# A conditioning layer on one core: other orders on VectorE and ScalarE, a weight block summed by TensorE, a last row scale without GpSimd

## The reference

```python
h = _ln(x, pw_g[pathway_ids], pw_b[pathway_ids])      # a row of 500 for each token
h = _ln(h, cp_g[compartment_ids], cp_b[compartment_ids])   # a row of 5
t = _ln(x, tm_g[time_steps], tm_b[time_steps])        # a row of 5
m = x + _mlp_ln(memory_state, ...)[:, None, :]        # n, r alike, one row a batch
s = _ln(x, ms_g[scale_type], ms_b[scale_type])        # a row of 3
w = softmax(aw)
cat = concatenate([w[0]*h, w[1]*t, w[2]*m, w[3]*n, w[4]*r, w[5]*s])   # 3072 features
out = x + _mlp_ln(cat, int_W1, int_b1, int_W2, int_b2, int_g, int_be)
```

## Time and profile before

| | |
|---|---|
| median of 3 runs | 950.84 us (950.79 to 952.48) |
| the profiled execution | 952.21 us, span of its instructions 950.5 us |
| mean granted clock of TensorE | 0.997 of full |
| PE, PEld busy | 923.2 us (97%), 745.4 us (78%) |
| DVE busy | 825.8 us (87%) |
| ACT, POOL busy | 326.0 us (34%), 449.8 us (47%) |
| L1567, L1568, L1569 (PE) | 397.1, 393.1, 392.9 us, 1008 matmuls each |
| L842 h_write | 60 DMAs of 256 KB from ACT's queue |

### The profile page before, as it was taken

The page is one execution under the profiler, slowest core; times in us unless marked ns, Lnnn a source line. Parts: engine busy times, 40 slices in busy tenths (PEclk is TensorE's granted clock), DMA queues, the critical chain, the costliest instruction groups (busy, mean ns, idle before and its releaser), DMA issues.

```text
span 950.5 us, 13455 instructions
## 1 busy us (share of the span) xinstructions
PE 923.2 (97%) x4166; PEld 745.4 (78%) x4166; DVE 825.8 (87%) x1199; ACT 326.0 (34%) x415; POOL 449.8 (47%) x576
## 2 busy tenths in 40 slices
...
GB/s 327 353 296 142 207 170 254 168 127 247 125 235 162 192 217 114 241 131 254 177 148 231 141 241 133 244 175 124 253 122 243 156 190 219 113 249 125 125 88 65
DMA packets 99618, 178.75 MB, mean 188 GB/s; under 512 B 10128, under 2 KB 49040, under 8 KB 95632
## 3 DMA queue, kind: packets, MB, share of 16 engines
...
...
## 4 chain that ended last, share of the span: by engine, by line
DVE 35%; issue 34%; PE 13%; POOL 11%; ACT 3%; DMA 2%; DVEq 1%; POOLq 1%; ACTq 0%; SPq 0%
DVE yst L1096 4%; DVE y_sb L1093 4%; DVE y_sb L1112 4%; DVE xc L1014 3%; DVE r_sb L1175 3%; DVE v_ring L1059 3%; PE hid_ps L1567 3%; PE hid_ps L1568 3%; PE hid_ps L1569 3%; POOL pw_rows L619 3%; DVE y_sb L1084 2%; POOL pw_rows L612 2%; POOL frs L541 2%; DVE fst L1128 2%; DVE cat_lo L1064 2%
## 5 line engine op out<-in xcount | busy, mean ns | idle before, releaser
L1567 PE MATMUL hid_ps<-cat_hi,w_hi 128*128 128x512 f32 x1008 | 397.1, 394 | 14.1 <-DVE cat_lo L1064 14.1
L1568 PE MATMUL hid_ps<-cat_lo,w_hi 128*128 128x512 f32 x1008 | 393.1, 390 | 0.0
L1569 PE MATMUL hid_ps<-cat_hi,w_lo 128*128 128x512 f32 x1008 | 392.9, 390 | 0.0
L1567 PEld LDWEIGHTS hid_ps<-cat_hi,w_hi 128*128 128x128 f32 x1008 | 189.5, 188 | 66.3 <-DVE cat_lo L1064 21.5
L1569 PEld LDWEIGHTS hid_ps<-cat_hi,w_lo 128*128 128x128 f32 x1008 | 189.6, 188 | 39.9
L1568 PEld LDWEIGHTS hid_ps<-cat_lo,w_hi 128*128 128x128 f32 x1008 | 189.7, 188 | 38.4
L612 POOL DMA_INDIRECT pw_rows<-pw,path_now x64 | 77.2, 1206 | 91.6 <-DVE y_sb L1112 75.4
L619 POOL DMA_INDIRECT pw_rows<-cp,class_now x64 | 93.4, 1459 | 36.8 <-issue 17.3
L633 POOL DMA_DIRECT2D r_sb<-x x60 | 57.3, 955 | 106.4 <-DVE r_sb L1175 103.3
L853 ACT ACTIVATE z_sb<-hid_ps,batch_bias 128x512 f32<-128x512 f32 x64 | 43.8, 691 | 168.9 <-PE hid_ps L1569 168.9
L835 ACT ACTIVATE cat_hi<-v_ring 128x1024 fp32r<-128x1024 f32 x30 | 31.9, 1062 | 154.1 <-DMA v_ring<-h_turned 154.1
...
## 6 DMA issues: line engine op xcount, KB each, us to landing
...
```

Of the source, the lines that this page charges most:

```text
L1567: pe.matmul(acc, w1_hi[:, k, cols], hi, start=start, stop=False)
L1568: pe.matmul(acc, w1_hi[:, k, cols], lo, start=False, stop=False)
L1569: return pe.matmul(acc, w1_lo[:, k, cols], hi, start=False, stop=stop)
```

## The change

It has five parts. In a steady batch (2 to 15) VectorE does `ts_mult`, `ts_low(b,0)`, both `hidden_low` and `ts_low(b,1)` before and between the `y_norm`, and the four `y_turn` in a row behind them; ScalarE does `ts_high(b,0)`, `(b,1)` before the last two `y_hat`, and `hinges(b,3)` ahead of `h_write`. In batch 1 one `ts_low` is moved. In the first batch block 1 of the x weights is summed by three fp32 matmuls with diagonal matrices that GpSimd makes (`block_sum`); `x_norm` goes from ScalarE to VectorE as one instruction with two scalars a row; seven warm-up matmuls go; and the order of the first list on both engines is another. At the end the row scale of the last 128 tokens comes from a root on ScalarE and four one-column steps on VectorE (a reciprocal and one step of Newton's method) instead of GpSimd's power.

```diff
@@ line 429 @@
 wait(sp, xhat_done, b - 1)
+if isinstance(b, int) and b == 1:
+    sp.wait_ge(block_summed, 1)
@@ line 543 @@
 wait(pool, pack_turned, b - 1)
-nth = 1 if isinstance(b, int) and b == 0 else b + 2
-rstd(xaggr, TT * (b + 1), xve, xve_done, xrs, xrs_done, xmv, slice(0, TT), nth)
+rstd(xaggr, TT * (b + 1), xve, xve_done, xrs, xrs_done, xmv, slice(0, TT), b + 1)
 if isinstance(b, int) and b == 0:
-    pool.wait_ge(xrs_done, 1)
-    pool.tensor_tensor(xmr[:, :], xmv[:, :, 0], xrs[:, :], ALU.mult).then_inc(xve_done, 1)
-    pool.wait_ge(xve_done, 2)
-    pool.tensor_tensor(xnmr[:, :], c_zero, xmr[:, :], ALU.subtract).then_inc(xrs_done, 1)
     return
 pool.nop(nofuse=True)
 pool.tensor_copy(x_pack[:, 0, :], xmv[:, :, 0]).then_inc(x_packed, 1)
-pool.wait_ge(xrs_done, b + 2)
+pool.wait_ge(xrs_done, b + 1)
@@ line 575 @@
 step(gain_bend, gain_mid, mid, ALU.subtract)
+pool.wait_ge(mix_ready, 1)
+for j in range(NETS):
+    pool.tensor_tensor(mix_diag[j], ident, w_mix[:, 2 + j:3 + j].to_broadcast([P, P]), ALU.mult).then_inc(diag_ready, 1)
@@ line 734 @@
 def sum_high(k):
-    act.wait_ge(sum_done, 2 * (k + 1))
-    act.activation(w1_hi[:, k, :], w1_raw[:, k, :], ACT.Copy).then_inc(sum_hi_done, 1)
+    if k == 1:
+        act.wait_ge(block_summed, 1)
+    else:
+        act.wait_ge(sum_done, 2 * SUMMED[k])
+    act.activation(w1_hi[:, k, :], made_ps[:, 1, :] if k == 1 else w1_raw[:, k, :], ACT.Copy).then_inc(sum_hi_done, 1)
@@ line 864 @@
 sum_high(0)
-sum_first(1)
 x_high(0, 1)
+sum_high(1)
 act.wait_ge(table_in, 16)
 act.activation(class_tab[:, :], tab_raw, ACT.Copy).then_inc(tab_rounded, 1)
 act.wait_ge(tab_rounded, 1)
 act.activation(class_tab[:, :], class_tab[:, :].bitcast(f32), ACT.Copy, scale=tab_sign).then_inc(tab_hi_done, 1)
-sum_high(1)
 sum_first(2)
-for t in range(TT):
-    x_norm(t)
@@ line 882 @@
 def first_chunk():
     w_high(4)
+    ts_high(0, 0)
     xhat_copy(1)
     w_high(5)
-    ts_high(0, 0)
     nets_rows()
     w_high(6)
     w_high(7)
@@ line 893 @@
 hinges(0, 3)
 w_high(8)
 w_high(9)
+ts_high(0, 2)
 nets_silu()
+ts_high(0, 3)
 w_high(10)
 w_high(11)
-ts_high(0, 2)
 w_high(12)
 w_high(13)
 w_high(14)
 w_high(15)
-ts_high(0, 3)
 for t in range(TT):
     y_hat(0, t)
 h_high(0, 0)
@@ line 939 @@
     y_hat(b, 0)
     y_hat(b, 1)
     hidden_high(b - 1, 1)
+    ts_high(b, 0)
+    ts_high(b, 1)
     y_hat(b, 2)
     y_hat(b, 3)
-    ts_high(b, 0)
-    ts_high(b, 1)
     hinges(b, 2)
+    hinges(b, 3)
     h_write(b)
-    hinges(b, 3)
     ts_high(b, 2)
     ts_high(b, 3)
 if first:
@@ line 973 @@
     last_hidden(h)
+act.activation(last_cols[:, 0:1], eps_col[:, 0:1], ACT.Sqrt).then_inc(root_tabled, 1)
+act.wait_ge(faggr, TT * BATCHES)
+act.activation(last_cols[:, 1:2], fmv[:, TT - 1, 1:2], ACT.Sqrt, bias=eps_col[:, 0:1]).then_inc(last_root, 1)
@@ line 1153 @@
 dve.wait_ge(out_ready, n - 2)
+if t < TT - 1:
+    dve.scalar_tensor_tensor(o_sb[:, t % 2, :], second_ps[t], fmv[:, t, 0:1], g_bc,
+                             ALU.subtract, ALU.mult).then_inc(fnum, 1)
+    return
+dve.tensor_tensor(fve[:, t:t + 1], fmv[:, t, 1:2], eps_col[:, t:t + 1], ALU.add).then_inc(last_var, 1)
 dve.scalar_tensor_tensor(o_sb[:, t % 2, :], second_ps[t], fmv[:, t, 0:1], g_bc,
                          ALU.subtract, ALU.mult).then_inc(fnum, 1)
+about, off, rest = [last_cols[:, i:i + 1] for i in range(2, 5)]
+dve.wait_ge(last_root, 1)
+dve.reciprocal(about, last_cols[:, 1:2]).then_inc(last_step, 1)
+dve.wait_ge(last_step, 1)
+dve.wait_ge(last_var, 1)
+dve.scalar_tensor_tensor(off, about, about, fve[:, t:t + 1], ALU.mult, ALU.mult).then_inc(last_step, 1)
+dve.wait_ge(last_step, 2)
+dve.tensor_scalar(rest, off, -0.5, 1.5, ALU.mult, ALU.add).then_inc(last_step, 1)
+dve.wait_ge(last_step, 3)
+dve.tensor_tensor(frs[:, t:t + 1], rest, about, ALU.mult).then_inc(frs_done, 1)
@@ line 1183 @@
     dve.wait_ge(sum_hi_done, k + 1)
-    dve.tensor_tensor(w1_lo[:, k, :], w1_raw[:, k, :], w1_hi[:, k, :].bitcast(f32),
+    dve.tensor_tensor(w1_lo[:, k, :], made_ps[:, 1, :] if k == 1 else w1_raw[:, k, :], w1_hi[:, k, :].bitcast(f32),
                       ALU.subtract).then_inc(sum_lo_done, 1)
+def x_norm(t):
+    dve.wait_ge(xrs_done, 1)
+    dve.tensor_scalar(x_sb[:, t, :], x_sb[:, t, :], xmv[:, t, 0:1], xrs[:, t:t + 1],
+                      ALU.subtract, ALU.mult).then_inc(x_normed, 1)
 def sum_blocks(k):
-    dve.wait_ge(sum_begun, k + 1)
+    dve.wait_ge(sum_begun, SUMMED[k])
     if k == 0:
         dve.wait_ge(sum_more_in[k], 16)
     for j in (1, 2):
         dve.scalar_tensor_tensor(w1_raw[:, k, :], keep[:, NETS * k + j, :], w_mix[:, 2 + j:3 + j], w1_raw[:, k, :],
                                  ALU.mult, ALU.add).then_inc(sum_done, 1)
-        dve.wait_ge(sum_done, 2 * k + j)
+        dve.wait_ge(sum_done, 2 * SUMMED[k] - 2 + j)
@@ line 1276 @@
     x_stats(0, t)
-sum_blocks(1)
 x_low(0, 1)
 sum_low(1)
+for t in range(TT):
+    x_norm(t)
@@ line 1287 @@
 ts_mult(0, 0)
 sum_low(3)
 w_low(4)
+ts_low(0, 0)
 w_low(5)
-ts_low(0, 0)
 ts_mult(0, 1)
 w_low(6)
 w_low(7)
 ts_low(0, 1)
-class_columns(True)
-y_mul(0, 0)
 ts_mult(0, 2)
 w_low(8)
 w_low(9)
+ts_mult(0, 3)
+ts_low(0, 2)
+class_columns(True)
 dve.wait_ge(tables_ready, 1)
-y_mul(0, 1)
-y_mul(0, 2)
-y_mul(0, 3)
-ts_low(0, 2)
+for t in range(TT):
+    y_mul(0, t)
+ts_low(0, 3)
 w_low(10)
 w_low(11)
 y_add(0, 0)
-ts_mult(0, 3)
 y_add(0, 1)
-ts_low(0, 3)
 y_add(0, 2)
 y_add(0, 3)
 w_low(12)
@@ line 1324 @@
 h_low(0, 1)
+nets_norm()
 class_rows()
-nets_norm()
@@ line 1348 @@
 y_norm(b, 1)
 ts_mult(b, 0)
 ts_mult(b, 1)
+ts_low(b, 0)
 y_norm(b, 2)
 y_norm(b, 3)
-ts_low(b, 0)
 ts_low(b, 1)
 ts_mult(b, 2)
 hidden_low(b - 1, 0)
@@ line 1360 @@
     ts_mult(b, 3)
     ts_low(b, 2)
 else:
+    y_norm(b, 0)
+    y_norm(b, 1)
+    ts_mult(b, 0)
+    ts_mult(b, 1)
+    ts_low(b, 0)
+    hidden_low(b - 1, 0)
+    y_norm(b, 2)
+    y_norm(b, 3)
+    hidden_low(b - 1, 1)
+    ts_low(b, 1)
     for t in range(TT):
-        y_norm(b, t)
-    hidden_low(b - 1, 0)
-    ts_mult(b, 0)
-    y_turn(b, 0)
-    ts_mult(b, 1)
-    y_turn(b, 1)
-    ts_low(b, 0)
-    y_turn(b, 2)
-    y_turn(b, 3)
-    ts_low(b, 1)
+        y_turn(b, t)
     ts_mult(b, 2)
-    hidden_low(b - 1, 1)
     ts_mult(b, 3)
     ts_low(b, 2)
 if not last:
@@ line 1602 @@
         pe.matmul(o_ps[:, 1, 0:P], sel_all, sel_all, start=True, stop=True)
+def block_sum():
+    pe.wait_ge(diag_ready, NETS)
+    pe.wait_ge(sum_in[1], 16)
+    for j in range(NETS):
+        ins = pe.matmul(made_ps[:, 1, :], mix_diag[j], keep[:, NETS + j, :], start=(j == 0), stop=(j == NETS - 1))
+    ins.then_inc(block_summed, 1)
@@ line 1672 @@
 pe.wait_ge(sel_ready, 1)
-warm(WARM[0])
+warm(WARM)
 x_high_part(0)
+block_sum()
 x_low_part(0)
-warm(WARM[1])
...
```

More of the change, by code:

```diff
@@ L29 @@
 FILLS0, FILLS = FT + 2, 2
-WARM = (24, 7)
+WARM = 24
 HI, LO, AGAIN, SCL = 0, 8, 16, 5
@@ L131, in build @@
         x_pack = pack_cols[:, 0:2 * TT].rearrange("p (s t) -> p s t", s=2)
-        xmr = sb("xmr", [P, TT])
-        xnmr = sb("xnmr", [P, TT])
         gain_tmp = sb("gain_tmp", [P, 7, FT])
@@ L149, in build @@
         frs = sb("frs", [P, TT])
+        last_cols = sb("last_cols", [P, 5])
         net_g = sb("net_g", [NR, D])
@@ L181, in build @@
         sel_all = v_ring[:, 3, 0, 2 * P:3 * P]
+        mix_diag = [stats_bc[:, j, 0:P] for j in range(NETS)]
         small_in = sem("small_in")
@@ L266, in build @@
         signs_ready = sem("signs_ready")
+        diag_ready = sem("diag_ready")
+        block_summed = sem("block_summed")
         hinged = sem("hinged")
@@ L299, in build @@
         last_stored = sem("last_stored")
+        root_tabled = sem("root_tabled")
+        last_root = sem("last_root")
+        last_var = sem("last_var")
+        last_step = sem("last_step")
         last_lo_done = sem("last_lo_done")
@@ L317, in add @@
             return len(tiles) - 1
+        SUMMED = {0: 1, 2: 2, 3: 3}
         SOURCE = {"h": 0, "t": 1, "s": 5}
```

11 lines of the change are left out of this document (3 added, 8 removed).

## The result

The changed kernel takes **968.62 us** (median of 4 runs, 967.83 to 969.22) against 951.55 us for the kernel before on the same chip: ratio 1.0178, 95% interval 1.0161 to 1.0196, 17 us slower. I had forecast 957.0 us and a range of 946 to 963. The direction was right and the time lies outside the range. The profiled execution took 967.83 us with a span of 966.1, against 950.5 before: +15.6 us, where my sum had +6.2.

What follows compares the result with a forecast made beforehand. VectorE was taken to pace the steady batches, with TensorE, though 97% busy, following. The terms -3.05 + 11.0 - 3.15 + 0.6 + 0.8 = +6.2 us gave 957.0 us from the 950.84 median; range 946 to 963.

Steps and rivals of the forecast that it cites:

- first batch: Start of the kernel: VectorE and TensorE both get into batch 1 earlier, -3.05 us (-1.9 with slower x_norm).
- 13 steady batches: Batches 2 to 15: ts_low(b,2) starts later behind h_write's issue, +0.85 us a batch, +11.0 us (3.2 to 12.6).
- earlier pair at TensorE, and its clock: Batch 15: TensorE's pair starts at T+5.36 instead of T+8.51, -3.15 us once; lowered clock after a stall, +0.8 us.
- the end: Last row scale: four dependent one-column VectorE steps, less 0.2 us idle, cost +0.6 us (0.4 to 0.9).
- the landing of h: Steady batches: h lands at T+26.8, y_mul wants it at T+27.04, 0.2 us spare; counted as nothing.
- early entries: First batch: block sum from 12.5 to 13.9, block 1's rounding ends at 15.5, block 2 starts at 21.2 (22.3).
- the stall at 50: First batch: a stall of 0.81 us and its restart, 0.97 in all, goes.
- the wait of 0.52 at 70.31: First batch: TensorE's wait there goes, as VectorE reaches x_low(1,0) at about 67.1 instead of 70.18.
- the issue: Steady batches: h_write's issue holds ScalarE's queue 3.73 to 3.90 us, delaying ts_high(b,2); +0.85 us a batch taken.
- Rival C: Steady batches: h's landing sets the pace, y_mul waits 1 us more a batch; +13, 970 us; chance 0.08.
- TensorE's waits: Sign in the profile after: TensorE's wait for cat_lo ahead of L1567 grows to about 25 us.

Runs made afterwards that it cites:

- e2: Kernel before with only the changed steady lists of VectorE and ScalarE (batches 2 to 15): 968.9 us, ratio 1.0171.
- e13: Repeat run of the kernel before with only the changed steady lists of VectorE and ScalarE: 974.3 us, ratio 1.0233.
- e1: Changed kernel with the steady lists of VectorE and ScalarE (batches 2 to 15) put back as before: 954.2 us, ratio 1.0022.
- e12: Changed kernel, h_write still on ScalarE's queue, with SyncE's loads of the first batch ordered by need: 966.0 us, ratio 1.0133.
- e7: Changed kernel with h_write on SyncE's queue and the middle of the first batch's VectorE and ScalarE lists as before (early y_mul): 933.6 us, ratio 0.9831.
- e8: Changed kernel with h_write on SyncE's queue and SyncE's loads of the first batch ordered by need: 932.2 us, ratio 0.9799.
- e14: Changed kernel with GpSimd's first residual add of a batch issued later, behind out_rstd(b-1,1): 958.9 us, ratio 1.0018.
- e6: Kernel before with only h_write's four DMAs moved to SyncE's queue: 934.3 us, ratio 0.9823.
- e10: Changed kernel with h_write on SyncE's queue, y_mul early, SyncE's loads by need, last row scale by GpSimd as before: 935.8 us, ratio 0.9819.
- e5: Changed kernel with h_write's four DMAs issued from SyncE's queue instead of ScalarE's: 936.9 us, ratio 0.9834.
- e3: Changed kernel with the last six side-net weight tiles loaded ahead of batch 1's loads on SyncE's queue: 969.5 us, ratio 1.0183.
- e15: Changed kernel unedited, run again for comparison on the same chip: 966.4 us, ratio 1.0096.
- e9: Changed kernel with SyncE's load of the next xT behind h_read in each batch instead of ahead: 963.4 us, ratio 1.0128.

## Why the prediction was wrong

The terms of the sum, against the traces of the two kernels:

| term | forecast | measured |
|---|---|---|
| first batch | -3.05 | +4.3 |
| 13 steady batches | +11.0 | +14.6 |
| earlier pair at TensorE, and its clock | -3.15 + 0.8 | -2.1 |
| the end | +0.6 | -1.2 |
| sum | +6.2 | +15.6 |

**Two steps failed**: the first batch, and the landing of h in the steady batches, which I had put at nothing. In this table the first is 7.3 us of the 9.4 that were missing, and the steady batches are 3.6. The experiments weigh them otherwise. The steady lists alone cost 17 us (e2, and by its ratio 22 in e13), where my steady terms make 8.65; the rest alone costs 2 us (e1), where I had -2.45; and in e12 an early first batch was followed by longer batches. So the two steps are not independent, and which part of the 9.4 us belongs to which stays open.

**The first batch**, "-3.05 us for both engines into batch 1", measured +4.28. Its early entries came out (block sum 12.62 to 14.87 against 12.5 to 13.9, block 1 at 16.21 against 15.5, block 2 at 21.57 against 21.2, the stall at 50 gone), and then the step followed only engines. The diff moved four `y_mul` behind `ts_mult(0,3)`, `ts_low(0,2)` and `class_columns`; I priced these as instructions and never asked what the last one releases: `load_x(1)` and the whole in-order queue behind it. e7 and e8 show it from two sides. Most of the 3.05 wasn't there either. With the crowd removed (e8) T(2) is 142.66, 0.9 us ahead of before on VectorE, and TensorE is not ahead at all: the same matmul of batch 1 starts at 86.93 us in before, 86.89 in e8, 87.07 in e7, and 91.24 in the changed kernel. The sum itself was loose here: its rows give TensorE 1.66 us and the wait of 0.52 at 70.31, some 2.2, and I booked VectorE's 3.1 for both engines.

**The steady batches**, +11.0, measured +14.6. For the issue the mechanism was right and its size too large: it gives 0.57 us a batch, 7.4 in all, not 0.85, since it took 3.60 us on average and the mean of before was T+16.66. What was missing is the landing, "I count nothing": h lands when expected (10.8 us behind the issue), but it is read back more slowly. The first `y_mul` now starts within 0.9 us of the landing, so the residual add and the read of h meet, and the second half comes late; 0.5 us a batch, 7 in all (e14). Rival C had the place wrong (`y_mul`, which waited for `h_turned` once, 0.8 us) and the direction right. That the two errors of this term, 3.6 us too much and 7 us missing, cancel in part is luck.

**The pair at TensorE and the clock**, -3.15 and +0.8, measured -2.1. The figure is that of TensorE's last matmul behind T(15), 64.31 and 62.21 us. The low part for the pair of batch 15 was ready at T+5.3, but TensorE came to it only at T+6.5: behind a wait of 2.80 us in batch 14 its clock was low.

```profile
...
845.00:850.00 5.00, 3.73 (x9) 2.96 (x10) 5.00 (x6) 2.86 (x4) 0.00 (x0) 0.56 0.23 90
850.00:855.00 5.00, 5.00 (x19) 3.98 (x18) 5.00 (x8) 2.25 (x4) 2.15 (x2) 0.75 0.31 44
...
```

The granted clock (the column behind the five engines) is 0.56 and 0.75 in the mean, so the lower of its two levels (1.2 of 2.4 GHz) held for most of 7 us; a pair takes 8.46 instead of 5.44 us: 3.0 us, where I had read 1.6. Of these 1.9 took the place of the wait that batch 15 would have had, and 1.1 are left. The same explains why TensorE's waits are 18.6 us and not 25: they stand in 10 batches and not in 14. Behind four of them (1.78, 2.72, 2.72 and 2.80 us) the pair took 7.2 to 8.5 us instead of 5.6, and the next batch's wait was shorter or gone. Behind one of 2.22 us it took 5.6.

**The end**, +0.6, measured -1.2. VectorE's four steps do cost 0.67 us from the last statistics to the last sum. But the span didn't end with VectorE. The end of GpSimd's queue, before and after (start at the right; duration in ns):

```profile
...
L58 POOLq DRAIN  x1: 5451/5451/5451, 944.8 to 944.8; - x1
...
```

```profile
...
L58 POOLq DRAIN  x1: 5447/5447/5447, 958.6 to 958.6; - x1
...
```

Before, the drain starts with the last power and ends at 950.3, 1.9 us behind SyncE's own drain at 948.4; after, GpSimd's last power is one tile earlier, its drain ends at 964.1, and SyncE's, at 965.9, is the last. From TensorE's last matmul to the end it is 7.07 us in before, e2, e6 and e10, whose last scale is GpSimd's, and 5.88 in after, e1 and e5.

**What stays open.** With the new steady lists a batch takes 58.1 to 58.4 us in e2, e12 and e13, where T(2) is 143 to 145, and 57.7 to 57.8 in after, e3 and e15, where it is 146 to 149. The excess sits at `h_low`, 1.4 to 1.5 against 0.8 to 0.9 us. In the traces the residual add is issued 0.5 to 0.8 us behind the start of the read in the first three and 1.0 us in the others; whether that makes the difference was not tried. And e9 and e14 were not run together with a repaired first batch.
